# Two constants of a list scheduler's cost model, and a store wait on VectorE, in an eight-core sequence-layer kernel

## What is computed

```python
n  = layernorm(x)
xc = causal_depthwise_conv(n, conv_w, 4 taps) + conv_b
r  = sigmoid(xc @ Wr.T + br);  i = sigmoid(xc @ Wi.T + bi)
a  = sigmoid(log_a) ** (8 * r)
b  = sqrt(clip(1 - a*a, 1e-6)) * (i * xc)
h  = exp(L) * cumsum(b * exp(-L)),  L = clip(cumsum(log(clip(a, 1e-7))), -80)
x  = x + layernorm(rmsnorm(h @ out_w.T) * norm_w)
m  = layernorm(x);  mp = m shifted by one token
xr = mu_r*m + (1-mu_r)*mp;  xk = mu_k*m + (1-mu_k)*mp
x  = x + layernorm(sigmoid(xr @ W_r.T) * (square(relu(xk @ W_k.T)) @ W_v.T))
```

## Time and profile before

| | us |
|---|---|
| median of 2 runs (1638.32 to 1638.45) | 1638.39 |
| the profiled execution, its own time | 1640.5 |
| its span on the slowest core (core 2) | 1639.0 |
| spans of the eight cores | 1628.0 to 1639.0 |
| TensorE matmul busy | 941.9 (57%) |
| VectorE busy | 933.6 (57%) |
| ScalarE busy | 795.5 (49%) |
| GpSimd busy | 15.7 (1%) |

### The profile page before, as it was taken

The page is one execution under the profiler, slowest core; times in us unless marked ns, Lnnn a source line. Parts: engine busy times, 40 slices in busy tenths (PEclk is TensorE's granted clock), DMA queues, the critical chain, the costliest instruction groups (busy, mean ns, idle before and its releaser), DMA issues.

```text
span 1639.0 us, 19878 instructions; the slowest of 8 cores (1628.0 to 1639.0 us)
## 1 busy us (share of the span) xinstructions
PE 941.9 (57%) x5713; PEld 581.4 (35%) x5762; DVE 933.6 (57%) x1506; ACT 795.5 (49%) x1287; POOL 15.7 (1%) x57
## 2 busy tenths in 40 slices
PE   0354748476483847558384656837464674847444
PEld 0132516143251615335161423515252442515212
DVE  0135665756666574755657475565657556564742
ACT  0553635456463645546363554636354563635422
POOL 1000000000000000000000000000000000000000
PEclk9986978779797968869797876969687796977758
DMA  9660010100101010010101000010100001010000
GB/s 137 128 95 1 1 52 1 52 1 1 52 1 52 1 52 1 5 48 1 52 1 52 1 26 26 1 52 1 52 1 35 18 1 52 1 52 1 26 0 26
DMA packets 21356, 47.46 MB, mean 29 GB/s; under 512 B 6912, under 2 KB 6912, under 8 KB 21248
## 3 DMA queue, kind: packets, MB, share of 16 engines
q1 hardware_dynamic: 14944, 33.59, 6.0%
q0 software_dynamic: 6304, 12.59, 5.0%
HBM read 41.99 MB, written 16.78 MB: 36 GB/s over the span
## 4 chain that ended last, share of the span: by engine, by line
PE 34%; DVE 33%; ACT 15%; issue 13%; SPq 2%; DVEq 1%; DMA 1%; ACTq 1%
PE PS L618 11%; PE PS L847 9%; PE PS L576 6%; DVE p L787 5%; DVE p L741 5%; DVE p L806 4%; PE PS L1008 3%; DVE p L753 3%; DVE xin L1115 2%; ACT p L627 2%; DVE p L655 2%; ACT p L690 2%; ACT p L763 2%; DVE vout L1108 2%; ACT PS L489 2%
## 5 line engine op out<-in xcount | busy, mean ns | idle before, releaser
L847 PE MATMUL PS<-w_ow,p 128*128 128x512 bf16 x511 | 147.8, 461 | 320.9 <-DVE p L806 290.6
L847 PEld LDWEIGHTS PS<-w_ow,p 128*128 128x128 bf16 x512 | 58.5, 114 | 410.0 <-issue 370.5
L618 PE MATMUL PS<-p,w_wi 128*128 128x256 bf16 x1024 | 181.5, 273 | 33.9 <-ACT p L627 33.8
L489 ACT ACTIVATE PS<-xin 128x1024 f32<-128x1024 f32 x64 | 65.8, 1028 | 261.3 <-DMA xin<-x 202.0
L618 PE MATMUL PS<-p,w_wr 128*128 128x256 bf16 x1024 | 180.8, 302 | 3.6 <-ACT p L593 2.4
L1077 PE MATMUL PS<-w_fv,p 128*128 128x512 bf16 x496 | 143.3, 453 | 64.7 <-DVE p L1057 57.0
L576 PE MATMUL PS<-ln1F,diag 128*128 128x256 bf16 x512 | 102.2, 368 | 126.2 <-ACT stats L504 120.8
L1039 PE MATMUL PS<-p,w_fk 128*128 128x256 bf16 x1024 | 140.6, 274 | 8.9 <-ACT p L627 5.4
L655 DVE TENSOR_TENSOR p<-p,c_loga 128x2048 f32<-128x2048 bf16 x16 | 36.7, 2292 | 177.8 <-ACT p L627 177.8
L1008 PE MATMUL PS<-w_fr,p 128*128 128x512 bf16 x480 | 131.1, 384 | 10.3 <-DVE p L982 7.4
L618 PEld LDWEIGHTS PS<-p,w_wi 128*128 128x128 bf16 x1024 | 99.1, 98 | 73.5 <-issue 46.7
(11 more groups left out here) (97 smaller groups left out, 1399.6 us busy)
## 6 DMA issues: line engine op xcount, KB each, us to landing
xin<-x SPq DMA_DIRECT2D x16, 1024.0 KB, 5.5
y<-xin SPq DMA_DIRECT2D x16, 1024.0 KB, 4.1
w_wr<-wr POOLq DMA_DIRECT2D x1, 2048.0 KB, 19.4
w_wi<-wi POOLq DMA_DIRECT2D x1, 2048.0 KB, 29.0
w_ow<-ow POOLq DMA_DIRECT2D x1, 2048.0 KB, 40.5
w_fr<-fr POOLq DMA_DIRECT2D x1, 2048.0 KB, 16.2
w_fk<-fk POOLq DMA_DIRECT2D x1, 2048.0 KB, 28.4
w_fv<-fv POOLq DMA_DIRECT2D x1, 2048.0 KB, 21.4
```

The costliest lines, as they stand in the source:

```text
L489: lambda e, s2=s, b=b, S_=S_, xap=xap, base=base: e.activation(bank2(b), xap[:, s2, :], AF.Square, bias=0.0, scale=1.0, accum_out=S_[:, ba ...
L618: lambda e, b=b, wn=wn, k=k, m=m, xcF=xcF: e.matmul(bank(b, CH), wsb[wn][:, k, m * 128:(m + 1) * 128], feat(xcF)[:, k, :], start=(k == 0), ...
L847: lambda e, b=b, k=k, s=s, half=half, hF=hF: e.matmul(bank(b), feat(hF)[:, k, s * 128:(s + 1) * 128], wsb["ow"][:, k, half * 512:(half + 1 ...
```

## The change

Two constants of the planner's cost model are raised, and one dependence is added: the four L1085 of a chunk, which write `vout`, now also depend on all stores issued up to that point of the code, those of the chunks before. The added dependence counts in the planner's priorities and times too, and puts one semaphore wait in front of the first L1085 of a chunk.

```diff
-COLD_WIN = 3400.0
+COLD_WIN = 4500.0
...
 def mm_est(nn):
-    return nn / 2.4 + (12 if WARM_MODEL else 45)
+    return nn / 2.4 + (20 if WARM_MODEL else 45)
...
-                        deps=[tmm, tok_rf[s * 2 + half]]
+                        deps=[tmm, tok_rf[s * 2 + half], ("DO", 16 * glob["nstores"])]
                              + glob["vout_lock"][c % N_VOUT] + vscr + lock4,
```

## The result

The changed kernel takes 1659.26 us (median of 7 runs, 1658.54 to 1692.08), the kernel before in the same job 1639.65 us (6 runs, 1638.32 to 1642.94). The 1692.08 is one execution in which the cores of one die ran at a lower granted clock; the others end at 1661.07. The ratio is 1.012, with an interval of 1.0107 to 1.0133. The prediction had 1659: slower by some 20 us, within 2% of before.

What follows compares the result with a forecast made beforehand. No engine bounds the kernel; a ring of handovers, passed once in each of 15 rounds, does. Terms 26.4 - 3.3 - 3.2 + 0.4 = +20.3 us on the median 1638.4 gave 1659 us, range 1636 to 1674.

Steps and rivals of the forecast that it cites:

- The table load dates the round: ScalarE's sigmoid table load: what moves ahead of it is paid or gained one for one, 15 times.
- The fourth eviction behind both L953: ScalarE's L593 moved: L618 waits for it, starting 1.83 us later in a high-clock round; 26.4 us with the early norm.
- the load at 832.65 or 834.24: Table load in the high-clock round: 1.85 us later if matmuls run at high clock, 3.44 us at low.
- The clock term: TensorE's sixteen matmuls from L618 to the load: four fifths of the way from 7.3 (high clock) to 31.2 us (low).
- The low round gains something first: Rounds with a slow convolution: L504 no longer waits behind an eviction; load +1.01 us at low clock, -0.58 at high.
- Pairs of `fr`: TensorE, `fr` pairs ahead of `wr` pairs: table load to L655 falls from 17.05 to 16.83 us, -3.3 us in all.
- The last full round: VectorE: L1115 leaves the way of the last `ow` product, a scan fills waiting ahead of L1085; together -3.2 us.
- The store wait: VectorE, ahead of L1085: never blocks, stores land long before; 0 to 0.8 us for 16 waits, 0.4 taken.
- A: Rival at L504 ahead of the first eviction: clock stays high, early norm wins, not slower; 1636 us, chance 0.14.
- B: Rival: low clock reaches behind the table load, 1.5 us more lost a round; 1682 us, chance 0.12.
- C: Rival: the change does nothing, lists differ only where nobody waits; 1638 us, chance 0.09.
- D: Rival: the wait for the stores blocks VectorE, tens of us lost if in each round; chance 0.01.

Runs made afterwards that it cites:

- the version that beats both: The changed kernel with only its fourth L593 put ahead of both L953 again: 1622.89 us, ratio 0.991.

## Why the prediction was right, step by step

**The table load dates the round: held.** All that the change cost lies between the convolution and that load, and L655 followed the load at a fixed distance in every kernel of the study (14 rounds at about 17.0 or 16.8 us by TensorE's order). The prediction's "over the 15 rounds 17.0 to 17.3 us" is true of 14; the last is 15.32. What it held at nothing is the way from L655 to the next L576, which fell by 3.5 us (6.0 in the mean of the eight cores), most of it in the `ow` product.

**The fourth eviction behind both L953: held, the split of its price did not.** I predicted L618 about 0.13 us behind the eviction; it is 0.14. From L930 to L618 the round above has 842.47 - 837.50 = 4.97 us. The step "the load at 832.65 or 834.24" forecast, at the four fifths taken, 23.4 us up to L618 and 3.0 us from L618 to the load, 26.4 together. Measured are 185.7 - 164.7 = 21.0 us from L576 to L618, and 6.2 us from there to the load, 27.2 together. The clock term was sized at half: I let it come back before the sixteenth matmul for a fifth of the way between the two ends, and it came back there in two rounds only, and late (3.49 or 3.50 us in 13 of the 15, 3.20 in the two others, at a mean granted clock of 0.59). The first part is off by two errors that go opposite ways. A high round loses 12.14 - 10.30 = 1.84 us from L576 to L618 and a low one 13.58 - 12.58 = 1.00, as forecast (1.83 and 1.01), but a middle one 12.14 - 10.03 = 2.11 and not 1.83; and three of the five low rounds became rounds of 12.14 us, which gives back 3 x 1.44 = 4.3 us. So the sum holds in part by luck. The same is true of the whole: the 3.5 us between L655 and L576, which the prediction didn't have, nearly cancel against the 2.65 us of the start. (The 31.2 us of the low end are 31.1 by their own terms.)

**The low round gains something first: right in mechanism, incomplete.** With only the norm moved, the kernel was 9.1 us faster. What I took as given was that 5 of 15 rounds have a slow convolution. In the changed kernel 2 have: the convolution takes 10.3 us less in all, and the stretch behind it 31.3 more. The two belong together. In the 13 other rounds the convolution takes anything from 6.11 to 6.77 us, and L618 still comes 12.14 us after L576 in 10 of them (12.15 to 12.47 in three), since the chain is the second norm, the transposes and ScalarE's list; a faster convolution only waits longer there. In the two slow rounds it is 13.58 us, and the convolution's end counts.

**Pairs of `fr`: held.** 16.80 us against 16.83 predicted; 14 rounds at -0.21 us. The last round went the other way, 15.32 to 15.97, and leaves -2.6 of the -3.3 us. Its list moved otherwise: the last pair of `wr` itself starts 14.33 us behind the table load (1532.45 - 1518.12) instead of 13.69 (1508.74 - 1495.05), which the prediction's "the last pair of `wr` does not move" missed.

**The last full round: held.** VectorE behind the last L655, as in the earlier trace rows:

```profile
1564.25 0.69 DVE L1085 SCALAR_TENSOR_TENSOR vout<-PS,p 128x512 f32<-128x512 f32 x1 [0.29 <-PE PS L1077]
...
1573.33 4.61 DVE L806 SCALAR_TENSOR_TENSOR p<-p,carryS,p 128x256 bf16<-128x256 f32 x8
1578.04 2.29 DVE L1115 TENSOR_TENSOR xin<-xin,vout 128x2048 f32<-128x2048 f32 x1
```

L1115 stands behind L806, and the wait ahead of L1085 is 0.29 us instead of 1.64. From the last L655 to the end of L806 it is 43.85 us instead of 46.93, which is -3.1; to the end of the program -3.2, as predicted.

**The store wait: held.** It was costed at 0.4 us from a handover of 0.05 us, which stands in none of the rows shown. The runs show nothing at all: 0.104 us ahead of the first L1085 with the wait and without, and two pairs of kernels (1642.34 beside 1639.92; 1621.41 beside 1625.74) that differ in opposite directions.

**The rivals.** *A* fell in the changed kernel, as L618 began high in no round. But its ingredients are real: the early norm alone gives 9 us, and with the clock kept up by fillers the changed kernel lies 5 us above the kernel before and not 20. That is not the price of the late eviction: the kernel with that eviction back in its place, and no fillers, takes 1622.89 us, 22 us less than the filled one. *B* fell: the stretch behind the load did not become longer. *C* fell with the timeline of ScalarE, *D* with the waits. Still open is the rounds' mix of slow and fast convolutions: no run forces it in the changed kernel, so that the -10.3 us (-7.8 in the mean of the eight cores) is a reading of one profiled execution and not a cause that was tried.

## What to carry to other kernels

On an engine that works in order, date an instruction by what waits for it and not by its own length: here 0.6 us of eviction, put behind two instructions that wait for TensorE, cost 40 us, and put back it made the change a gain. A planner that is given other constants can improve some places (here the early norm, the `fr` pairs and the last full round) and spoil one more, so look at the places one by one before the total is believed. And before a stage is made faster, look at the rounds in which the next stage waits for it: 38 us off the convolution brought 7.

## What the runs showed of the hardware that was not expected

**A short idle of TensorE can cost its clock for what comes next, and a few matmuls keep it.** With transposes only in a stretch of 3.5 us, 4 of 15 rounds began L618 at 1.00 (2.4 GHz) and the others at or soon after at 0.50 (1.2 GHz). The transposes of the high round at 829 us themselves ran at 1.00, from 827.48 on. In the changed kernel, where TensorE also stands idle for 2.2 to 2.8 us behind them, all 15 rounds began the first gate group at 0.50, and 13 ran its sixteen matmuls at 0.50 to the end. With six matmuls of 1.46 us in that idle time, 12 of 15 rounds ran it at 1.00. The Trainium skill, TensorE: Matmul & The Clock Gate, Part 4 (PE-mode transpose), says that transposes don't count as busy time in the way of other matmuls. The 15 low starts of the changed kernel agree with it; the four high rounds of the kernel before do not bear it out in full.

**A gain of clock in one stage moves the clock of the next.** The number of rounds with a slow convolution was 5 before, 2 after, 2 in the version that beats both, and 8 when fillers sped up the product ahead of it; over the eight cores the means are 2.8, 1.0, 1.6 and 7.9. None of these kernels changes the convolution. The last step was forced by the fillers; the first three are as they fell out. A few us of such a total are therefore a matter of the mix, and only kernels with the same order upstream can be compared more finely.

**The table load waits with its activation.** The 1.28 us of the load would fit twice into the 3.64 us for which ScalarE idles ahead of it, but in the traces it starts only when the first gate group is done, for which its sigmoid waits. It lies on the path, and so does everything that dates the first gate group.
